# A graph network with sorted chains: held rows and running sums as scans over features in PSUM

## The chip, the cores and the metric

One core of a Trainium2 chip. The time is device time of the whole kernel in microseconds (us); smaller is better. Engines: TensorE (PE), VectorE (DVE), ScalarE (ACT), GpSimd (POOL), SyncE (SP, which only issues DMAs here).

## The reference, cut to what matters

6,250 nodes with 128 features, 100,000 edges sorted by destination. Four graph layers, each followed by a layer norm over nodes:

```python
# layer 0 ("first walk")
theta = x[dst] - x[src]
w = sigmoid(relu(theta @ W1 + b1) @ W2 + b2)
agg = segment_sum(w * theta, dst)
# layer 1: attention over edges grouped by source (needs the edges sorted by source: "sort" and "sorted pass")
# layer 2 ("transformer's walk"), 8 heads of 16
scores = sum(q[src] * k[dst], -1) / 4 + edge_attr @ We + be
ex = exp(scores - segment_max(scores, dst)[dst]); agg = segment_sum(v[src] * ex / den[dst], dst)
# layer 3: two graph attention layers, 4 heads of 32 ("attention walks")
```

## The kernel before, in words

**Chains.** Each of the 128 partitions holds 784 consecutive edges; a walk goes through them in 56 groups of 14 edges (`NG`, `B`). `cont[:, e]` is 1 where edge e has the same destination as the edge before it, otherwise 0. A segment sum is a running sum multiplied by `cont`: the sum at a node's last edge is the node's, and is fetched from `states` in HBM afterwards. A destination's row likewise is written by an indirect DMA at its first edge only (`spread_wide`, zero elsewhere) and *held* along the chain: held(e) = held(e-1) * cont(e) + row(e).

**A group of a walk.** POOL issues 14 indirect gathers, one per edge slot, each of 128 table rows into `rows` (L707), two groups in turn. It waits for `idx_staged` (ACT copies the indices, L1214) and for `rows_used` of the group two before. SP loads the group's spread rows into `dstf` (L580) once `dst_used` says that the held rows two groups back are made. DVE (function `turn`) computes scores, ACT the exponentials (and, in the first walk, 14 rows times their weight, L1196), DVE adds up, ACT saves the group's 14 rows of sums to `states` (L1223), two buffers in turn.

**First walk** (phase 0). DVE: subtract held - row, relu times W2 (one `stt`), from group `M0` = 20 on two bf16 one-hot compares for a histogram of sources (`mark_sources`), reduce; ACT exp; DVE 1/(1+..); ACT weighs row by row into `gated` in PSUM and tells `msg_ready` in parts; DVE then interleaves 14 adds into `sums` with 14 `hold` operations for the next group, each one `scalar_tensor_tensor` over 128 features that depends on the one before it:

```python
m = stt(S3[:, j, 0:A], prev, same_chain(g)[:, j:j + 1], part[:, j * A:(j + 1) * A], ALU.mult, ALU.add)
m = stt(held[:, j, :], prev, same_chain(g)[:, j:j + 1], dstf[:, s, j, 0:D], ALU.mult, ALU.add)
```

**Transformer's walk** (phase 2): the same with q*k product, reduce by head, two scans for the running maximum, exp on ACT, messages (v times exp, 136 wide with the denominators) into `msgp`, then the same 14 + 14 interleaved operations.

**Sort** (phase 1, `sort_edges`, `place_edges`, `hold_row`, ACT's `payloads`): for every group DVE builds bf16 one-hots (`build`), PE counts, DVE picks each edge's place, ACT copies the held rows (132 wide), weight and source number into `payload`, and POOL scatters 14 times 128 payloads to HBM (`by_src`, L634). It needs `payload_ready` and `place_ready`; ACT needs `sort_out`, the landing of the scatters of two groups before. DVE's hold operations for the next group stand among and behind the picks and wait for `held_copied`. After group 2 DVE also folds weights.

**Attention walks** (phases 3 and 4) already work the other way, and the change takes their form: a PSUM tile with the feature outside and the slot inside, 15 slots per feature (slot 0 the carry), a gate tile of the same shape with `cont` in slots 1 to 14 and 0 in slot 0, and one `tensor_tensor_scan` over all of it (L2057); ACT turns the result back into `sums` (L1217) and writes the next gate (L1179).

Line numbers of helpers in the profile: L1260 `tt`, L1268 `cp`, L1271 `stt`, L1274 `red`.

Of the kernel before, what the change touches and what calls it, by code (L numbers as in the profile page):

```python
# [7 lines left out]
ALU = mybir.AluOpType  # L8
# [56 lines left out]
def build(nc, a, out):  # L65
    with ExitStack() as ctx:  # L66
# [186 lines left out]
        gated = psA[:, 2 * D:(B + 2) * D]  # L253
# [3 lines left out]
        chain_exq = psA[:, 2048:2048 + 4 * (B + 1)]  # L257
        held = psA[:, 2048:2048 + B * D].rearrange("p (b d) -> p b d", d=D)
        heldS = psA[:, 0:B * ROW].rearrange("p (b d) -> p b d", d=ROW)
# [11 lines left out]
        w2p = psA[:, 2048 + B * D:2048 + B * D + D]  # L271
# [28 lines left out]
        gates_ready = sem("gates_ready")  # L300
        states_turned = sem("states_turned")
# [26 lines left out]
        base_ready = sem("base_ready")  # L328
# [7 lines left out]
        msg_ready = sem("msg_ready")  # L336
        hold_step = sem("hold_step")
# [101 lines left out]
        MSG_PARTS = [1, 5, 9, 13]  # L439
# [283 lines left out]
        def _(pe):  # L723
# [88 lines left out]
            for ph in range(5):  # L812
# [114 lines left out]
                if ph == 0:  # L927
                    pe.matmul(psX[:, 0:F], chains[0][:, :], last[:, 0:F], start=True, stop=True).then_inc(st_carry, 1)
# [18 lines left out]
        def _(act):  # L947
# [40 lines left out]
            def payloads():  # L988
# [3 lines left out]
                act.wait_ge(src_in, 48)  # L992
                for g in range(NG):
# [4 lines left out]
                    act.activation(payload[:, s, :, 0:ROW].rearrange("p b (h d) -> p b h d", d=33)[:, :, :, 0:32],  # L998
                                   heldS[:, :, 0:D].rearrange("p b (h d) -> p b h d", d=32), ACT.Copy)
                    act.activation(payload[:, s, :, ROW:ROW + 4], heldS[:, :, D:ROW], ACT.Copy).then_inc(held_copied, 1)  # L1000
# [38 lines left out]
            for ph in range(6):  # L1039
# [133 lines left out]
                else:  # L1173
                    act.wait_ge(rows_used, 2 + TURN[ph] * NG)
                    for s in range(2):
                        act.activation(idx[:, s, :], src[:, s * B:(s + 1) * B], ACT.Copy).then_inc(idx_staged, 1)
                def chain_gates(g):
# [3 lines left out]

                if ph >= 3:
                    act.wait_ge(n_stage, KG * (ph + 1))
                    act.wait_ge(n_kept, 3 * KG)
                    chain_gates(0)
                for it in range(IT if ph != 1 else 0):
                    for s in range(2):
                        g = it * 2 + s
                        act.wait_ge(scores_ready, g + (1 + ph * NG))
# [1046 lines left out]
```

## Time and profile before

| | |
|---|---|
| median of 3 runs | 6638.7 us (6636.5 to 6639.4) |
| the profiled execution | 6635.3 us, span 6633.5 us |
| DVE / POOL / ACT / PE busy | 4655 / 4292 / 1376 / 1265 us |
| first walk, first to last gather | 244 to 1254 us |
| sort, first to last scatter | 1456 to 2473 us |
| transformer's walk | 3111 to 4098 us |
| attention walks | 4388 to 5374, 5533 to 6519 us |

DVE is the engine with the largest share; the stages named above follow one another, with node updates (gathers of sums, projections, layer norms) between them. An indirect DMA is counted as busy on POOL for the time in which POOL issues it.

### The profile page before, as it was taken

Reading aid. Unit: us, or ns where it says so; the run is one execution under the profiler, and the core shown is the slowest. Engines: PE = TensorE matmul, PEld = TensorE weight load, DVE = VectorE, ACT = ScalarE, POOL = GpSimd, SP = SyncE. Lnnn points to the kernel's source line nnn. Section 1 sums busy time; section 2 is a strip of 40 time slices with the busy share of each in tenths; the row PEclk is TensorE's granted clock in tenths of the full one; section 3 lists DMA queues with packets and bytes.
Section 4 is the critical chain, followed back from the end, with each engine's and each line's share of the span. In section 5 each row is a group of like instructions: output and inputs, shape, how many; then the busy total and the mean of one; then the engine's idle time right before and its main releaser. Section 6 shows DMA issues by size and latency. Waiting matters only on the chain. (4 is left out here: it accounts for less than half of the span.)

```text
span 6633.5 us, 37157 instructions
## 1 busy us (share of the span) xinstructions
PE 1264.7 (19%) x8049; PEld 1104.1 (17%) x8049; DVE 4654.6 (70%) x9454; ACT 1375.5 (21%) x3580; POOL 4291.5 (65%) x4445
## 2 busy tenths in 40 slices
PE   7100000145555534332000000820000010000000
PEld 6100000134554433322000000620000010000000
DVE  7678888799999969976888887644444443444445
ACT  0122222221111114431000000522222211222223
POOL 0677777667777760016777775457777767777775
PEclk9655555555555555556555555855555555555555
DMA  9666666434444437744666665123333323333332
GB/s 373 188 211 211 202 202 202 136 102 132 134 132 134 132 115 293 294 174 132 219 217 221 221 219 169 32 72 109 114 109 111 113 79 90 109 112 111 109 114 82
DMA packets 338944, 1032.97 MB, mean 156 GB/s; under 512 B 100325, under 2 KB 163137, under 8 KB 331294
## 3 DMA queue, kind: packets, MB, share of 16 engines
q0 software_dynamic: 166752, 401.68, 21.2%
q1 hardware_dynamic: 116642, 342.34, 14.8%
q10 hardware_dynamic: 55324, 286.57, 12.0%
q8 instruction: 63, 1.03, 0.1%
q14 instruction: 163, 1.34, 0.1%
HBM read 602.97 MB, written 427.39 MB: 155 GB/s over the span
## 5 line engine op out<-in xcount | busy, mean ns | idle before, releaser
L707 POOL DMA_INDIRECT rows<-table,idx x3136 | 2986.7, 952 | 982.6 <-issue 972.2
L634 POOL DMA_INDIRECT by_src<-ebuf,place x784 | 771.0, 983 | 274.6 <-issue 238.4
L1271 DVE SCALAR_TENSOR_TENSOR psA<-psA,cont,dstf 128x128 f32<-128x128 f32 (+1 forms) x2349 | 836.5, 356 | 52.0 <-ACT ebuf L1000 31.3
L1260 DVE TENSOR_TENSOR sc<-rows,ebuf 128x56 f32<-128x56 f32 x112 | 28.2, 252 | 1023.5 <-DMA rows<-table,idx 1023.5
L933 PE MATMUL psA<-dstf,ones 128*128 128x512 f32 x10 | 9.9, 1113 | 3055.9 <-DVE dstf L2176 3055.9
L1271 DVE SCALAR_TENSOR_TENSOR sums<-sums,cont,psA 128x128 f32<-128x128 f32 (+1 forms) x1512 | 519.3, 343 | 30.5 <-ACT psA L1196 29.1
L933 PEld LDWEIGHTS psA<-dstf,ones 128*128 128x128 f32 x10 | 2.7, 315 | 3057.5 <-issue 3057.5
L802 PE MATMUL psA<-attr,sums 128*128 128x49 f32 x1568 | 406.0, 403 | 474.8 <-DVE attr L1449 474.8
L2057 DVE TENSOR_TENSOR_SCAN psA<-rows,psA 128x1980 f32<-128x1980 f32 x112 | 480.1, 4287 | 3.9
L802 PEld LDWEIGHTS psA<-attr,sums 128*128 128x128 f32 x1568 | 396.9, 326 | 480.9 <-DVE attr L1449 480.9
L1202 ACT ACTIVATE psA<-df 128x60 f32<-128x60 f32 (+1 forms) x168 | 40.4, 241 | 1714.5 <-DVE df L1260 1714.5
L1260 DVE TENSOR_TENSOR psA<-rows,psA 128x1848 f32<-128x1848 f32 (+1 forms) x168 | 352.7, 2100 | 0.0
L714 POOL DMA_INDIRECT fixr<-states,fixi x5 | 5.0, 998 | 518.3 <-DMA states<-sums 464.5
L653 POOL DMA_INDIRECT spread_wide<-rows,nidx x147 | 153.4, 1044 | 267.4 <-DVE rows L1260 219.4
L1260 DVE TENSOR_TENSOR rows<-rows,psA 128x1792 bf16<-128x1792 bf16 (+3 forms) x121 | 234.4, 1937 | 108.4 <-DMA rows<-table,idx 104.7
L645 POOL DMA_INDIRECT sums<-states,nidx x245 | 256.7, 1048 | 81.2 <-issue 73.1
L1260 DVE TENSOR_TENSOR rows<-psA,rows 128x1792 f32<-128x1792 f32 (+2 forms) x168 | 203.1, 1210 | 124.1 <-DMA rows<-table,idx 112.6
L1217 ACT ACTIVATE sums<-psA 128x1848 f32<-128x1848 f32 x112 | 191.7, 1711 | 460.0 <-DVE psA L2057 460.0
L998 ACT ACTIVATE ebuf<-psA 128x1792 f32<-128x1792 f32 x56 | 94.2, 1682 | 907.5 <-DMA by_src<-ebuf,place 788.1
L1196 ACT ACTIVATE psA<-rows,wt 128x128 f32<-128x128 f32 x784 | 232.9, 352 | 33.7 <-DVE wt L2077 33.7
L774 PE MATMUL psA<-ebuf 128*128 128x49 bf16 x504 | 54.4, 276 | 971.7 <-DVE ebuf L1260 971.7
L803 PEld LDWEIGHTS psA<-rows 128*128 128x128 bf16 x784 | 210.2, 268 | 0.0
(336 smaller groups left out, 5409.4 us busy)
## 6 DMA issues: line engine op xcount, KB each, us to landing
dstf<-spread_wide SPq DMA_DIRECT2D x168, 924.0 KB, 7.0
states<-sums ACTq DMA_DIRECT2D x150, 952.0 KB, 3.9
rows<-by_src SPq DMA_DIRECT2D x55, 1035.0 KB, 5.1
states<-sums ACTq DMA_DIRECT2D x56, 1008.0 KB, 5.8
spread_wide<-sums SPq DMA_DIRECT2D x56, 924.0 KB, 24.3
states<-sums ACTq DMA_DIRECT2D x56, 903.0 KB, 7.2
rows<-table,idx POOLq DMA_INDIRECT x3136
msg<-low_rows SPq DMA_DIRECT2D x56, 448.0 KB, 3.8
```

The lines of the kernel that those rows point to most:

```text
L634: pool.indirect_dma_start(by_src[:, :], bass.IndirectOffsetOnAxis(ap=place[:, s, j:j + 1], axis=0), payload[:, s, j, :], None).then_inc(so ...
L645: pool.indirect_dma_start(nrows[g % NS][:, b * w:(b + 1) * w], None, states[ph - 1][:, :], bass.IndirectOffsetOnAxis(ap=nidx[:, order, k:k ...
L653: pool.indirect_dma_start(spread[ph][:, :], bass.IndirectOffsetOnAxis(ap=nidx[:, 1, k:k + 1], axis=0), zslot(ph, g)[:, b * ZW[ph]:(b + 1) ...
L707: pool.indirect_dma_start(rows[:, at:at + GW[ph]], None, table[ph][:, :], bass.IndirectOffsetOnAxis(ap=idx[:, s, j:j + 1], axis=0)).then_i ...
L802: pe.matmul(t, hotT[s][:, j, :], cell[:, :, j], start=True, stop=False)
L803: m = pe.matmul(t, same[s][:, j, :], hotH[s][:, :, j], start=False, stop=True)
L998: act.activation(payload[:, s, :, 0:ROW].rearrange("p b (h d) -> p b h d", d=33)[:, :, :, 0:32], heldS[:, :, 0:D].rearrange("p b (h d) -> ...
L1196: m = act.activation(gated[:, j * D:(j + 1) * D], rows[:, at:at + D], ACT.Copy, scale=wt[:, s, j:j + 1])
L1217: act.activation(S3[:, :, 0:F], chain_msg.rearrange("p (f b) -> p b f", b=B + 1)[:, 1:B + 1, :], ACT.Copy).then_inc(states_turned, 1)
L1260: return dve.tensor_tensor(o_, a_, b_, op)
L1271: return dve.scalar_tensor_tensor(o_, a_, s_, b_, op0, op1)
L2057: tell(dve.tensor_tensor_scan(chain_msg, chain_gate, chain_msg, 0.0, ALU.mult, ALU.add), su)
```

## The change

In the first walk, the sort and the transformer's walk:

- `hold_row` and `hold` go. ACT copies the group's spread rows from `dstf` into a PSUM tile turned by feature (slots 1 to 14), after it has copied slot 14 of the group before into slot 0, and writes a gate from `cont`. DVE runs two scans, each over half the features.
- The 14 adds go. In the first walk ACT weighs its 14 rows straight into slots 1 to 14 of `first_acc`, and `msg_ready` in parts is gone: the sums begin when all 14 are weighed. In the transformer's walk DVE writes the messages turned. DVE adds up in two scans of half the features; ACT then turns the sums into `sums` in SBUF and only then saves them.
- In the first walk the order on DVE is: hold scans of the next group, then sum scans. In the transformer's walk the front half of the hold scans comes ahead of the messages, the back half behind the sum scans.
- The gates are bf16 in the walks (64 or 68 features x 15) and f32 in the sort (66 x 15). The transformer's exponentials lie in PSUM from column 3968, in its last bank.
- New waits: the histogram's matmuls wait for the states of the group before (`states_turned0`), and ACT's weighing waits for the histogram's matmuls.

```diff
-        gated = psA[:, 2 * D:(B + 2) * D]
+        wide_msg = psA[:, 0:(B + 1) * 136]
+        wide_held = psA[:, 2048:2048 + (B + 1) * D]
+        wide_exq = psA[:, 3968:3968 + 8 * (B + 1)]
+        acc_gate = msg[:, 0:(B + 1) * 34].bitcast(BF16)
+        hold_gate = msg[:, (B + 1) * 34:(B + 1) * 66].bitcast(BF16)
+        sort_held = psA[:, 0:(B + 1) * ROW]
+        first_held = psA[:, 0:(B + 1) * D]
+        first_acc = psA[:, 2048:2048 + (B + 1) * D]
...
                     pe.wait_ge(hist_ready, g + 1)
+                    pe.wait_ge(states_turned0, g)
...
+                def turn_held(g):
+                    act.wait_ge(dst_landed[g % 2], 16 + 16 * IT + 16 * (g // 2))
+                    if g:
+                        act.activation(view[:, :, 0], view[:, :, B], ACT.Copy).then_inc(hold_carried, 1)
+                        act.wait_ge(hold_carried, NG - 1 + g)
+                        act.wait_ge(held_copied, g)
+                        act.activation(view[:, :, 1:B + 1].rearrange("p f b -> p b f"), dstf[:, g % 2, :, :], ACT.Copy)
...
+                    act.activation(sort_gate.rearrange("p (f b) -> p f b", b=B + 1)[:, :, 1:B + 1],
+                                   cont[:, g * B:(g + 1) * B].unsqueeze(1).to_broadcast([P, 66, B]), ACT.Copy).then_inc(hold_turned, 1)
...
+                        if ph == 0 and g < NG - 1:
+                            turn_first(g + 1)
+                        if ph == 2 and g < NG - 1:
+                            turn_held(g + 1)
                         act.wait_ge(scores_ready, g + (1 + ph * NG))
...
+                            act.wait_ge(hist_used, max(g + 1, M0))
                             for j in range(B):
-                                m = act.activation(gated[:, j * D:(j + 1) * D], rows[:, at:at + D], ACT.Copy, scale=wt[:, s, j:j + 1])
-                                if j in MSG_PARTS[:-1]:
-                                    m.then_inc(msg_ready, 1)
+                                m = act.activation(acc_rows[:, :, j + 1], rows[:, at:at + D], ACT.Copy, scale=wt[:, s, j:j + 1])
...
+                        if ph == 0:
+                            act.wait_ge(sums_saved[s], it * 16 + 16)
+                            m = act.activation(sums[:, s * B * W:(s + 1) * B * W].rearrange("p (b w) -> p b w", b=B)[:, :, 0:D],
+                                               acc_rows[:, :, 1:B + 1].rearrange("p f b -> p b f"), ACT.Copy)
+                            if g < NG - 1:
+                                m = act.activation(acc_rows[:, :, 0], acc_rows[:, :, B], ACT.Copy)
+                            m.then_inc(states_turned0, 1)
+                            if g < NG - 1:
+                                first_gate(1, g + 1).then_inc(sum_gates, 1)
+                            act.wait_ge(states_turned0, g + 1)
...
+            def hold_turn(g):
+                half = 66 * (B + 1)
+                dve.wait_ge(hold_turned, NG + g + 1)
+                dve.tensor_tensor_scan(sort_held[:, 0:half], sort_gate, sort_held[:, 0:half], 0.0, ALU.mult, ALU.add)
+                dve.tensor_tensor_scan(sort_held[:, half:2 * half], sort_gate, sort_held[:, half:2 * half],
+                                       0.0, ALU.mult, ALU.add).then_inc(dst_used, 1)
...
                 cp(place[:, s, :], spot[:, :]).then_inc(place_ready, 1)
-                if held_next:
-                    for j in range(3, B):
-                        hold_row(holds, g + 1, j)
+                if g < NG - 1:
+                    hold_turn(g + 1)
...
+                            if ahead:
+                                hold_first(g + 1)
+                            dve.wait_ge(rows_used, g + 3)
+                            dve.wait_ge(sum_gates, g + 1)
+                            for k in range(2):
+                                m = dve.tensor_tensor_scan(halves_of(first_acc)[k], first_gates[1], halves_of(first_acc)[k], 0.0, ALU.mult, ALU.add)
+                            tell(m, su)
...
+                            if ahead:
+                                hold_front(g + 1)
+                            wide_messages(g, G3, Sp)
+                            if ahead:
+                                hold_back(g + 1)
```

## Rows read from the trace of the kernel before

**Rows 1.** The page: busy time, share of the span, instructions of each engine.

```profile
PE 1264.7 (19%) x8049; PEld 1104.1 (17%) x8049; DVE 4654.6 (70%) x9454; ACT 1375.5 (21%) x3580; POOL 4291.5 (65%) x4445
```

**Rows 2.** Windows by stage: stretch, length, engines' busy us (xcount), clock, DMA share, GB/s.

```profile
700.00:1200.00 500.00, 40.82 (x378) 35.01 (x378) 424.23 (x988) 126.68 (x434) 374.85 (x382) 0.50 0.61 201
1700.00:2400.00 700.00, 357.56 (x2716) 345.46 (x2716) 647.35 (x979) 77.56 (x156) 532.47 (x544) 0.50 0.41 134
3200.00:4000.00 800.00, 0.00 (x0) 0.00 (x0) 691.06 (x1626) 44.96 (x227) 601.49 (x636) 0.50 0.67 221
4500.00:5200.00 700.00, 0.00 (x0) 0.00 (x0) 311.76 (x315) 166.83 (x276) 526.34 (x559) 0.50 0.38 111
```

**Rows 3.** Lines, first walk: xcount, busy us, mean ns, idle before and its releasers.

```profile
L707 POOL DMA_INDIRECT rows<-table,idx x784 | 759.0, 968 | 251.0 <-issue 241.2 <-ACT idx L1214 7.6 <-ACT psA L1196 2.1
```

**Rows 4.** Timeline, first walk, group 25: start us, us, engine, line, tiles, idle before.

```profile
705.43 2.02 DVE L1260 TENSOR_TENSOR rows<-psA,rows 128x1792 f32<-128x1792 f32 x1 [1.32 <-DMA rows<-table,idx]
...
713.92 4.16 ACT L1196 ACTIVATE psA<-rows,wt 128x128 f32<-128x128 f32 x14 [0.59 <-DVE wt L2077]
...
721.84 0.33 ACTq L1223 DMA_DIRECT2D states<-sums  x1
...
723.36 2.03 DVE L1260 TENSOR_TENSOR rows<-psA,rows 128x1792 f32<-128x1792 f32 x1 [1.28 <-DMA rows<-table,idx]
```

**Rows 5.** Timeline, transformer's walk, two group starts on DVE.

```profile
3611.41 2.02 DVE L1260 TENSOR_TENSOR rows<-rows,psA 128x1792 f32<-128x1792 f32 x1 [7.57 <-DMA rows<-table,idx]
...
3627.36 2.02 DVE L1260 TENSOR_TENSOR rows<-rows,psA 128x1792 f32<-128x1792 f32 x1
```

**Rows 6.** Timeline, sort, one group of ACT and DVE.

```profile
1970.94 1.68 ACT L998 ACTIVATE ebuf<-psA 128x1792 f32<-128x1792 f32 x1 [16.85 <-DMA by_src<-ebuf,place]
...
1972.76 0.36 DVE L1271 SCALAR_TENSOR_TENSOR psA<-psA,cont,dstf 128x132 f32<-128x132 f32 x1 [1.62 <-ACT ebuf L1000]
...
1979.30 0.24 DVE L1268 TENSOR_SCALAR psA<-attr 128x49 f32<-128x49 f32 x1
...
1981.40 1.52 DVE L1260 TENSOR_TENSOR rows<-digits,ebuf 128x1792 bf16<-128x1792 bf16 x2
```

**Rows 7.** Sort: the waits (total us, times, longest), and the scatters by line.

```profile
DVE psA L1271 <- ACT ebuf L1000: 31.3, 42, 1.9
...
L634 POOL DMA_INDIRECT by_src<-ebuf,place x784 | 771.0, 983 | 274.6 <-issue 238.4 <-DVE place L1268 36.2
```

**Rows 8.** Timeline, POOL's issues beside the pair of one-hot compares, three places.

```profile
933.70 1.59 DVE L1260 TENSOR_TENSOR ebuf<-digits,ebuf 128x1792 bf16<-128x1792 bf16 x2
933.74 0.94 POOL L707 DMA_INDIRECT rows<-table,idx  x1 [0.30 <-issue]
...
1674.75 1.51 DVE L1260 TENSOR_TENSOR rows<-digits,ebuf 128x1792 bf16<-128x1792 bf16 x2
1674.80 1.86 POOL L634 DMA_INDIRECT by_src<-ebuf,place  x1 [0.30 <-issue]
...
1982.46 1.29 POOL L634 DMA_INDIRECT by_src<-ebuf,place  x1 [0.30 <-issue]
```

**Rows 9.** Timeline, sort, POOL waiting for place numbers.

```profile
1514.21 0.96 POOL L634 DMA_INDIRECT by_src<-ebuf,place  x1 [4.42 <-DVE place L1268]
```

**Rows 10.** Lines, attention walk, 4400 to 5370 us: two scans and ACT's turn.

```profile
L2057 DVE TENSOR_TENSOR_SCAN psA<-rows,psA 128x1980 f32<-128x1980 f32 x55 | 235.8, 4287 | 1.9
...
L1217 ACT ACTIVATE sums<-psA 128x1848 f32<-128x1848 f32 x55 | 94.1, 1711 | 225.9 <-DVE psA L2057 225.9
...
L2093 DVE TENSOR_TENSOR_SCAN fm<-nf,sc 128x60 f32<-128x60 f32 x55 | 15.5, 282 | 2.2 <-DVE sc L1271 0.4
```

**Rows 11.** Timeline, end of the first walk: weighing and save.

```profile
1266.00 4.16 ACT L1196 ACTIVATE psA<-rows,wt 128x128 f32<-128x128 f32 x14 [0.59 <-DVE wt L2077]
...
1272.59 0.33 ACTq L1223 DMA_DIRECT2D states<-sums  x1
```

**Rows 12.** Timeline, end of the transformer's walk: the dependent adds.

```profile
4109.33 5.06 DVE L1271 SCALAR_TENSOR_TENSOR sums<-sums,cont,psA 128x136 f32<-128x136 f32 x13
```

More of the change, by code:

```diff
@@ L438, in build @@
         XS = [1, 1, 1, 3, 1, 0]
-        MSG_PARTS = [1, 5, 9, 13]
         @block.sync
@@ L1201, in _ @@
                             n = H * (B + 1)
-                            act.activation((chain_exq if ph >= 3 else exq)[:, 0:n], df[:, 0:n], ACT.Exp).then_inc(weights_ready, 1)
+                            act.activation((chain_exq if ph >= 3 else wide_exq)[:, 0:n], df[:, 0:n], ACT.Exp).then_inc(weights_ready, 1)
                             act.wait_ge(sums_saved[s], it * 16 + (16 + 16 * IT * TURN[ph]))
@@ L1441, in build, with place_edges @@
                 dve.wait_ge(built, g + 3)
-            def place_edges(holds, g):
+            def place_edges(g):
                 s = g % 2
@@ L2009, in _ @@
                         link(dve.memset(chain_gate.rearrange("p (f b) -> p f b", b=B + 1)[:, :, 0], 0.0))
-                    link(dve.memset(held[:, B - 1, :], 0.0)) if ZW[ph] == ROW else None
-                    link(cp(w2p, bias[:, bb("L0_gnn_W2"), :])) if ph == 0 else None
+                    if ph == 2:
+                        for gate in (acc_gate, hold_gate):
+                            link(dve.memset(gate.rearrange("p (f b) -> p f b", b=B + 1)[:, :, 0], 0.0))
+                    if ph == 0:
+                        for gate in first_gates:
+                            link(dve.memset(gate.rearrange("p (f b) -> p f b", b=B + 1)[:, :, 0], 0.0))
+                        link(dve.memset(first_acc.rearrange("p (f b) -> p f b", b=B + 1)[:, :, 0], 0.0))
+                        tell(cp(w2p, bias[:, bb("L0_gnn_W2"), :]), hrd)
                     link(dve.memset(mx[:, :], 0.0))
@@ L2016, in _ @@
                 sr = Steps(scores_ready, NG * ph)
-                holds = Steps(hold_step, (B - 1) * NG * min(ph, 2))
-                accs = Steps(acc_step, (B - 1) * NG * ph)
-                parts = Steps(msg_ready)
+                mxd = Steps(held_read, NG + 1)
                 wide = int(ZW[ph] == ROW)
-                part, A = (msgp, F) if ph else (gated, D)
+                part, A = msgp, F
                 def same_chain(g):
                     return cont[:, g * B:(g + 1) * B]
-                def hold(g, j, first=False):
-                    s = g % 2
-                    prev = held[:, j - 1, :] if j else held[:, B - 1, :]
-                    if j:
-                        dve.wait_ge(hold_step, holds.value())
-                    if first and j == 0:
-                        m = cp(held[:, 0, :], zrow[:, 0:D])
-                    else:
-                        m = stt(held[:, j, :], prev, same_chain(g)[:, j:j + 1], dstf[:, s, j, 0:D], ALU.mult, ALU.add)
-                    if j < B - 1:
-                        m.then_inc(hold_step, 1)
-                        holds.add()
-                    else:
-                        m.then_inc(dst_used, 1)
-                        du.add()
                 def turned_messages(g, G3, Sp):
@@ L2136, in turn @@
-                        dve.wait_ge(sums_ready, su.value())
-                        if wide and ahead:
-                            dve.wait_ge(dst_used, du.value())
+                            if ahead:
[3 more added lines that the diff above has]
+                                hold_back(g + 1)
                 wr = Steps(weights_ready)
@@ L2145, in _ @@
                         link(ts(hb(nf)[:, :, 1:B + 1], same_chain(0).unsqueeze(1).to_broadcast([P, H, B]), -1.0, ALU.add, BIG, ALU.mult))
-                    if wide:
-                        dve.wait_ge(dst_landed[0], 16 + 16 * IT * ph)
-                        dve.wait_ge(zfirst_in, 16 * (ph + 1))
-                        for j in range(B):
-                            hold(0, j, first=True)
-                        dve.wait_ge(dst_used, du.value())
+                    if ph == 2:
+                        hold_front(0)
+                        hold_back(0)
+                    if ph == 0:
+                        hold_first(0)
                     for it in range(IT):
@@ L2168, in _ @@
                     continue
-                if ph >= 3:
-                    dve.wait_ge(states_turned, (ph - 2) * NG)
+                dve.wait_ge(states_turned, (ph - 1) * NG) if ph > 1 else None
                 if ph > 1:
```

185 lines of the change are left out of this document (111 added, 74 removed).

## The prediction, made before the change was run

> **What bounds the kernel now.** I read the page's engine shares first: DVE is busy for 70% of the span, GpSimd (POOL) for 65% [rows 1]. That points at DVE; the windows by stage correct it [rows 2]. POOL issues 636 gathers in 800 us of the transformer's walk and 559 in 700 us of an attention walk: 1.258 and 1.252 us each, so 14 of them, a group, take 17.5 to 17.6 us. The rate is the same where DVE is busy for 86% and for 45%. In the first walk from group 20 on it is 1.309 us, in the sort 1.287. The listing by line agrees: of 251.0 us in which POOL stands idle in the first walk, 241.2 are its own 0.30 between issues [rows 3]. So POOL's issue of 14 indirect DMAs a group sets the pace of all these stages, and DVE's share is high only because its work nearly fills that time.
>
> How nearly, the timeline tells. In the first walk DVE starts a group at 705.43, ends its adds at 721.8 and its last held row 0.26 later, and waits 1.3 us for the rows of the next at 723.36 [rows 4]: a chain of 16.7 us in 17.9. Before group 20 the pair of histogram compares (1.3 us) is missing: 15.4. In the transformer's walk the chain is 15.95 us (3611.41 to 3627.36) [rows 5]. In the sort, groups come every 18.0 us (1.287 x 14) and DVE waits in 42 of them, 0.75 us each, for ACT's payload copies [rows 7]: a chain of about 17.2. ACT in turn had waited 16.85 us for scatters of two groups earlier to land [rows 6]; so POOL leads there too.
>
> What slows POOL in two stages is visible as well. An undisturbed issue takes 0.96 us in the sort and 0.946 in the walks, the mean is 0.983 and 0.968: over 784 issues 18 to 20 us and 17 us [rows 3, 7]. The long ones lie under the pair of bf16 one-hot compares, DVE instructions with both inputs in SBUF, and their price hangs on where POOL stands when the pair starts [rows 8]: an issue that falls 1.06 us behind the pair's start (1982.46 behind 1981.40) takes 1.29, one 0.05 us behind takes 1.86, one 0.04 us behind takes 0.94. So the price climbs to 0.90 as the issue comes nearer to the start, and falls off an edge between 0.05 and 0.04. The Trainium skill (SBUF — State Buffer, section Who interferes with whom) infers that a tensor_tensor takes only the shared read interface and leaves descriptor writing alone; by that these delays would be 0 wherever the pair starts. The rows show 0.90, so I go by the rows. A third loss: POOL once waits 4.42 us for DVE's place numbers behind the weight folds [rows 9], and 9.7 us for ACT in the first walk, a few times about 2 [rows 3].
>
> **The change, part by part.** Scan cost first: 1,980 elements take 4.287 us, 60 take 0.282 [rows 10], so 2.086 ns an element and 0.157 us fixed; 960, 990 and 1,020 elements take 2.16, 2.22 and 2.28 us, and two with no wait between them overlap by 0.08. ACT: 1,848 elements in 1.711 us, 128 every 0.30 [rows 4, 10]: 0.82 ns each and 0.19 fixed. A turn of 1,792 elements takes 1.68, a gate of 896 0.93, of 924 0.95, of 952 0.97, a carry 0.30. An ACT instruction starts 0.1 before the end of an independent one ahead of it.
>
> *First walk.* DVE loses 28 row operations, 7.4 us at a spacing of 0.26, and gains four scans of 960 elements, 4.23 + 4.23 us. The chain to the weights stays (713.92, +8.5) [rows 4]. ACT turns the next destination rows under the compares and the reduce: held tile free at +4.1, carry, turn and gate 2.9, done at +7.1, before the scores at +7.6. Hold scans run +8.7 to +12.9, while ACT weighs 14 rows (4.16, done at +12.65), sum scans to +17.2. Chain 17.2 us against 17.9: hidden, by 0.7. Before group 20 the scores are there at +6.2 but ACT at +7.1, so the exponential comes 1.0 later: 15.4 + 0.5 + 1.0 = 16.9 against 17.5, hidden. POOL needs the rows freed by +15.9 (its next group ends 17.8 us after the last gather, rows land 1.9 after it); they are free at +12.7. The added waits: the next subtract stands behind the hold scans (+12.9), the histogram matmuls behind the previous turned states, ACT's weighings behind those matmuls (done by +7.2, needed at +8.5), the save of states behind a turn, a carry and a gate. The save goes out 3 us later, the destination load 4 us earlier than now (both at 721.8 to 722.1 [rows 4]); gathers that land beside both come late (7.57 us of waiting [rows 5]). I take 0 for that; bounds: POOL's waits for ACT go (-6 to -10), or later landings shift the compares' price in 36 groups by -0.3 to +0.4 us (-11 to +14).
>
> The last group has no cover. Now the adds begin with the first weighed row, and the save leaves 6.6 us after the weights, at 1272.59 [rows 11]. After: 4.16, two scans 4.23, turn 1.68 and 0.1 of waits, 10.2 in all: **+3.7 us**, on the path, since POOL waits for that save.
>
> *Transformer's walk.* Hold front (2.16) starts when the maxima are done at +5.6 and also covers the 0.44 of waiting for the exponential; then carry product, messages 2.14, two scans of 1,020 (4.48), hold back 2.16: 5.6 + 2.2 + 0.2 + 2.2 + 4.5 + 2.2 = 16.9 us against 17.6, hidden by 0.7. ACT's turn of the held rows ends at +5.1, before +5.6. At the end, 14 dependent adds of 5.4 us [rows 12] become scans of 4.48 and a turn of 1,904 elements, 1.76: **+0.9 us**.
>
> *Sort, start and stall.* The copy and 13 dependent holds (5.5 us at the spacing of [rows 12]) become two scans of 990 (4.36) behind an ACT turn that fits under build(0): -0.8, if the load has landed. In each group DVE loses three interleaved rows and eleven dependent ones and gains 4.36 us: 17.2 becomes 16.7, place numbers come 0.4 earlier within the group. The first scatter waits for DVE and so does the one behind the stall [rows 9]: 0.8 + 3 x 0.5 + 0.4, **-2.7 us**.
>
> *Sort, steady part.* DVE keeps ahead of POOL, but the place where its cycle is tied to POOL moves. Now: scatters land, ACT starts the payload at 1970.94 (call it T), DVE resumes at T+1.82 and the compares start at T+10.46 [rows 6]. After: the payload's four copies end at T+2.0, the carry at T+2.2, the turn of 1,848 at T+3.9, the gate at T+4.8; DVE T+4.9, scans 4.36, cell copy T+9.3, compares 2.10 later as in [rows 6], at T+11.43: 0.97 us later. POOL's beat of 1.26 stays, so the issue that now falls 1.06 behind the compares' start will fall 0.09 behind it: just short of the edge, where the price is 0.86 instead of 0.33. Of some 47 steady groups I take 35 at 0.84, 12 beyond the edge at 0.3, and 8 early ones at 0.5: 37 us against today's 19, **+18 us**. Bounds: all beyond the edge, 11 us (-9); all short of it, 45 (+25).
>
> Sum: +3.7 - 2.7 + 18 + 0.9 = +19.9 us. The profiled execution took 6635.3 us (span 6633.5), 3.4 under the median of 6638.7; it becomes 6655, the median **6658 us**.
>
> The skill (VectorE: DVE Perf Modes, section The TRN2 errata) says that small VectorE operations pay a fixed cost each and recommends 512 elements or more, which speaks for 4 instructions instead of 28. Here the scans' 2.09 ns an element eats that up, and with POOL in front neither would move the end.
>
> **Rivals.** (B) *The compares slip past the edge.* It needs the sort's ACT chain to be 0.05 us longer than I have it. Collisions 11 us instead of 19, all else as above: +1.9 - 9 = -7, median 6632; with groups on either side, up to +13. For: how little separates 0.09 from 0.04. Against: the chain is built from measured durations. (C) *ACT or DVE becomes the bound in a walk.* If ACT's copies into a PSUM tile with a step of 15 elements take twice as long (+1.7 us), the exponential of the first walk and hold front of the transformer's come about 1.2 us late: chains of 18.0, 18.4 and 18.1 against 17.5, 17.95 and 17.6, so 20 x 0.5 + 36 x 0.45 + 56 x 0.5 = 54 us on the forecast, 6712; it decides above 0.6 us more a group. Against: reading PSUM with that step is at full rate (1.711 for 1,848 [rows 10]). (D) *Faster:* gathers no longer land beside save and load together. POOL's waits go (-6), later landings slip the histogram's compares past their edge (36 x 0.3 = -11), the sort's slip too (-9), with -2.7 and +4.6: -24 us, 6615. It decides once landings shift by 0.5 us. Against: two independent slips. (E) *Nothing measurable:* the collisions stay: +1.9, 6641.
>
> **How the numbers follow.** A measurement of this kernel tells 0.2%, 13 us, from no change. My forecast case has 0.55, of which 0.44 lies above +13 and 0.11 below; B and E together 0.30, within; C 0.07, slower; D 0.08, faster. So faster 0.08, same 0.41, slower 0.51. The forecast case alone runs from +5 to +32 (6644 to 6671); for eight in ten I reach down over B and up into C: 6629 to 6682.
>
> **What would show it.** Right: issues still every 1.25 us with 0.30 idle; DVE chains near 17.2, 16.9 and 16.7 us; mean scatter near 1.005 us instead of 0.983, with an issue about 0.1 us behind the compares' start; save of the last first-walk group 3.7 us later behind its weights; the stall of 4.42 some 2 us shorter. Wrong: DVE without waits for rows over whole stretches (C); mean scatter at 0.98 or below (B, E); mean gather of the first walk under 0.96 and no wait of POOL for ACT (D).

## The result, and the profile after the change

The changed kernel takes 6653.9 us (median; 6647.3 to 6657.5), the kernel before 6638.1 on the same chip: a ratio of 1.0023, 95% interval 1.0017 to 1.0029. The profiled execution spans 6652.9 us instead of 6633.5: **+19.4 us**, where the sum of the prediction had +19.9. For this pair of executions the sum is right to half a microsecond, its terms are not; the medians differ by 15.8 us.

The page after the change, and the windows over the stretches of [rows 2] in the same columns:

```profile
PE 1263.5 (19%) x8049; PEld 1102.1 (17%) x8049; DVE 4744.1 (71%) x6098; ACT 2140.7 (32%) x4363; POOL 4298.5 (65%) x4445
```

```profile
700.00:1200.00 500.00, 42.35 (x392) 36.30 (x392) 443.70 (x326) 276.36 (x597) 372.01 (x381) 0.50 0.61 201
1700.00:2400.00 700.00, 353.61 (x2677) 341.62 (x2677) 625.25 (x501) 181.55 (x266) 535.42 (x534) 0.50 0.41 131
3200.00:4000.00 800.00, 0.00 (x0) 0.00 (x0) 744.95 (x545) 293.25 (x455) 601.53 (x635) 0.50 0.67 220
4500.00:5200.00 700.00, 0.00 (x0) 0.00 (x0) 312.14 (x315) 167.27 (x280) 526.84 (x559) 0.50 0.38 111
```

DVE issues 3356 instructions fewer and is busy for 90 us more (a scan of 960 elements costs 2.14 us); ACT is busy for 765 us more. In the transformer's walk DVE goes from 691 to 745 us of 800, and POOL still issues 635 gathers there (636 before). What changed in time is read from the starts and ends of POOL's first and last issue of each stage:

| stage | before, us | after, us | difference |
|---|---|---|---|
| ahead of the first walk | 244.4 | 246.0 | +1.6 |
| first walk, 784 gathers | 1009.6 | 1018.0 | +8.4 |
| last gather to the fix of the chunk ends | 22.9 | 24.9 | +2.0 |
| from there to the first scatter | 178.8 | 177.5 | -1.3 |
| sort, 784 scatters | 1016.9 | 1025.5 | +8.6 |
| transformer's walk, 784 gathers | 987.3 | 987.1 | -0.2 |
| all the rest | 3173.6 | 3173.9 | +0.3 |

*The sort.* One steady group in the timeline, ACT, DVE and POOL (start, us, engine, line, tiles, idle before); the answer to [rows 6]:

```profile
2054.44 1.69 ACT L1027 ACTIVATE ebuf<-psA 128x1792 f32<-128x1792 f32 x1 [13.85 <-DMA by_src<-ebuf,place]
...
2056.65 1.71 ACT L1013 ACTIVATE psA<-dstf 128x1848 f32<-128x1848 f32 x1
2058.30 0.96 ACT L1018 ACTIVATE rows<-cont 128x924 f32<-128x924 f32 x1
...
2047.15 1.52 DVE L1357 TENSOR_TENSOR rows<-digits,ebuf 128x1792 bf16<-128x1792 bf16 x2
...
2059.29 2.23 DVE L1513 TENSOR_TENSOR_SCAN psA<-rows,psA 128x990 f32<-128x990 f32 x1 [1.99 <-ACT rows L1018]
...
2065.98 1.51 DVE L1357 TENSOR_TENSOR rows<-digits,ebuf 128x1792 bf16<-128x1792 bf16 x2
...
2046.06 0.95 POOL L643 DMA_INDIRECT by_src<-ebuf,place  x1 [0.30 <-issue]
2047.32 1.76 POOL L643 DMA_INDIRECT by_src<-ebuf,place  x1 [0.31 <-issue]
```

The payload starts at 2054.44 (T), the scans at T+4.85, the compares at T+11.54; predicted were 4.9 and 11.43 (over the steady groups the compares start at T+11.36 in the median, in the kernel before at T+10.47). In the group before, the compares start at 2047.15 and the next issue falls 0.17 behind and takes 1.76. Of 40 steady groups (from 1700 us on) 28 have this issue 0.07 to 0.18 behind the compares, at 0.79 to 0.91 us above the undisturbed 0.96. The line of the scatters and POOL's stall, against [rows 7, 9]:

```profile
L643 POOL DMA_INDIRECT by_src<-ebuf,place x784 | 781.3, 997 | 271.8 <-issue 238.5
...
1522.73 0.95 POOL L643 DMA_INDIRECT by_src<-ebuf,place  x1 [2.63 <-DVE place L1365]
```

997 ns instead of 983 over 784 scatters are the sort's +10.3 us, and the stall gives back 1.8.

*The first walk.* A group start, and POOL's longest waits at groups 9, 18, 27, 36, 45 and 54, each ahead of the third gather:

```profile
712.55 2.02 DVE L1357 TENSOR_TENSOR rows<-psA,rows 128x1792 f32<-128x1792 f32 x1 [1.09 <-DMA rows<-table,idx]
...
408.54 0.95 POOL L716 DMA_INDIRECT rows<-table,idx  x1 [2.86 <-issue]
...
569.00 0.94 POOL L716 DMA_INDIRECT rows<-table,idx  x1 [3.25 <-issue]
732.77 0.94 POOL L716 DMA_INDIRECT rows<-table,idx  x1 [4.18 <-issue]
899.23 0.94 POOL L716 DMA_INDIRECT rows<-table,idx  x1 [3.84 <-issue]
1065.49 0.94 POOL L716 DMA_INDIRECT rows<-table,idx  x1 [3.89 <-issue]
...
1230.22 0.94 POOL L716 DMA_INDIRECT rows<-table,idx  x1 [3.83 <-issue]
```

The same six waits are in the kernel before, at 1.21 to 1.31 us (one of them below), and in the transformer's walk of both, at about 1.3; in the attention walks they take 1.0 to 1.1.

```profile
725.20 0.94 POOL L707 DMA_INDIRECT rows<-table,idx  x1 [1.25 <-issue]
```

In the first walk of the changed kernel they grew by 14.3 us together, while the waits for ACT went from 9.7 to 5.6 (the first walk's line: mean gather 966 ns, idle 260.5 us instead of [rows 3]'s 251.0). Nothing in the prediction names this pause.

### The profile page after: what moved, and what is told of

Same layout as the page of the kernel before. It is cut to its first block and busy times, and to the rows that moved or that the text cites. A ratio compares the mean times of both kernels' runs of the same rounds, so it can differ in the third digit from the quotient of the medians.

```text
span 6652.9 us, 34825 instructions
## 1 busy us (share of the span) xinstructions
PE 1263.5 (19%) x8049; PEld 1102.1 (17%) x8049; DVE 4744.1 (71%) x6098; ACT 2140.7 (32%) x4363; POOL 4298.5 (65%) x4445
## 3 DMA queue, kind: packets, MB, share of 16 engines
q14 instruction: 145, 1.19, 0.1%
## 5 line engine op out<-in xcount | busy, mean ns | idle before, releaser
L2160 DVE TENSOR_TENSOR_SCAN psA<-msg,psA 128x960 f32<-128x960 bf16 x112 | 234.5, 2140 | 8.0 <-ACT msg L1210 8.0
L2192 DVE TENSOR_TENSOR_SCAN psA<-msg,psA 128x960 f32<-128x960 bf16 x112 | 234.1, 2136 | 3.9 <-ACT psA L1280 3.9
```

The source lines that it names most:

```text
L2160: m = dve.tensor_tensor_scan(halves_of(first_held)[k], first_gates[0], halves_of(first_held)[k], 0.0, ALU.mult, ALU.add)
L2192: m = dve.tensor_tensor_scan(halves_of(first_acc)[k], first_gates[1], halves_of(first_acc)[k], 0.0, ALU.mult, ALU.add)
```

## The experiments

Times are medians beside the kernel before on the same chip. "Sort" is the time from the first scatter's start to the last's end, "first walk" the same of its gathers.

| run | us | before | ratio (95%) | first walk | sort | mean scatter, ns |
|---|---|---|---|---|---|---|
| the change | 6653.9 | 6638.1 | 1.0023 (1.0017 to 1.0029) | 1018.0 | 1025.5 | 997 |
| e1, gate early | 6630.1 | 6636.7 | 0.9991 (0.9982 to 1.0000) | 1012.5 | 1009.5 | 977 |
| e2, 0.08 us later | 6647.9 | 6636.7 | 1.0017 (1.0008 to 1.0026) | 1014.1 | 1025.9 | 997 |
| e3, load late | 6638.8 | 6636.7 | 1.0004 (0.9995 to 1.0013) | 1004.6 | 1025.3 | 997 |
| e4, half the descriptor space | 6687.6 | 6636.7 | 1.0077 (1.0062 to 1.0092) | 1016.1 | 1035.3 | 998 |
| e5, gate early, turn in three | 6631.1 | 6639.6 | 0.9988 (0.9979 to 0.9997) | 1016.0 | 1003.9 | 969 |
| e6, turn in three | 6636.5 | 6639.6 | 0.9995 (0.9986 to 1.0004) | 1016.2 | 1008.4 | 975 |
| e7, e5 and e3 | 6619.4 | 6639.6 | 0.9970 (0.9957 to 0.9982) | 1005.3 | 1004.8 | 970 |
| e8, before, one copy split | 6632.0 | 6639.6 | 0.9989 (0.9980 to 0.9998) | 1013.6 | 1008.9 | 973 |

**What sets the price of the sort's scatters?** First the gate is moved ahead, so that the compares start earlier:

```diff
+                    if g < NG - 1:
+                        held_gate(g + 1)        # ahead of the payload copies
...
                     if g < NG - 1:
                         turn_held(g + 1)        # the turn alone
```

> After the change, with ACT's gate of the sort's next group written as soon as DVE's scans of this group are done, ahead of the payload copies instead of behind the turn. Theory (the place of the compares on POOL's beat sets the price of an issue): the compares start about 0.85 us earlier in each steady group, so the issue that follows them falls about 0.95 instead of 0.1 us behind their start; by the prices of the two traces that is 0 to 0.33 us a group instead of 0.80 to 0.90. Mean scatter 0.97 to 0.983 instead of 0.997, 6640 to 6645 us, 9 to 14 below the change. Rival (the scans themselves, or the gates that they read from SBUF, slow the scatters): mean scatter stays at 0.997 and the time within 3 us of the change.

A steady group of e1, compares and the issues beside them:

```profile
2034.68 1.52 DVE L1364 TENSOR_TENSOR rows<-digits,ebuf 128x1792 bf16<-128x1792 bf16 x2
...
2034.55 0.96 POOL L643 DMA_INDIRECT by_src<-ebuf,place  x1 [0.30 <-issue]
2035.81 1.22 POOL L643 DMA_INDIRECT by_src<-ebuf,place  x1 [0.30 <-issue]
```

The sort is 16.0 us shorter and the scatters' mean is 977: the theory holds, the rival (scans or gates slow the scatters) falls, since both are still there. The compares moved 0.89 us earlier behind the payload's start (median), and the issue now falls 1.13 us behind their start instead of 0.17. The median is 10 us below the range that was expected. In the profiled executions the other 5.5 us come from the first walk, which e1 doesn't touch. So that walk varies from run to run: five runs with the change's own first walk (the change, e1, e2, e5, e6) gave 1012.5 to 1018.0, mean 1015.4, and the two with that of before 1009.6 and 1013.6. By these means the walk's +8.4 would be nearer to +4.

Then the other way, by one more small ACT copy ahead of the turn (e2), and by splitting the turn (e6):

```diff
+                        act.activation(...sort_gate..., [:, 0:1, 1:B + 1], ... cont ..., ACT.Copy)      # e2
```

```diff
-                        act.activation(view[:, :, 1:B + 1]..., dstf[:, g % 2, :, :], ACT.Copy)
+                        for f in range(0, ROW, 44):                                                   # e5, e6, e7
+                            m = act.activation(view[:, f:f + 44, 1:B + 1]..., dstf[:, g % 2, :, f:f + 44], ACT.Copy)
```

> After the change, with one more small ACT copy (the gate's first feature written twice, 14 elements, 0.1 to 0.2 us) between the payload and the turn of the sort's held rows. Theory of the place on the beat: the compares start 0.1 to 0.2 us later, past the start of the next issue; the issues that cost 0.80 to 0.90 in some 28 groups cost about 0.16 to 0.33: mean scatter 0.97 to 0.98, 6636 to 6643 us, 11 to 18 below the change although only work was added. Rival (the chain over ACT and DVE is what costs): the time is the change's or up to 10 us above, since each group gets 0.15 us longer.

> The change with the gate where the change has it and the turn of the sort's held rows in three copies, 0.16 to 0.2 us later than the change, about twice what one small copy added (0.08 us, which left the next issue 0.05 to 0.07 us behind the compares' start, still short of the edge, at 0.89). Theory of the place on the beat: now the issue starts just ahead of the compares, price 0.16 to 0.24 instead of 0.8 to 0.9: mean scatter 0.970 to 0.980, 10 to 16 us below the change's 6652: 6636 to 6642 us. Rival (the longer chain costs): 6652 to 6660 us.

One group of e2, then one of e6:

```profile
2045.12 1.52 DVE L1360 TENSOR_TENSOR rows<-digits,ebuf 128x1792 bf16<-128x1792 bf16 x2
...
2045.19 1.85 POOL L643 DMA_INDIRECT by_src<-ebuf,place  x1 [0.30 <-issue]
```

```profile
2038.73 1.53 DVE L1358 TENSOR_TENSOR rows<-digits,ebuf 128x1792 bf16<-128x1792 bf16 x2
...
2038.72 0.96 POOL L643 DMA_INDIRECT by_src<-ebuf,place  x1 [0.30 <-issue]
2039.98 1.12 POOL L643 DMA_INDIRECT by_src<-ebuf,place  x1 [0.30 <-issue]
```

e2's expected gain did not come: the copy moved the compares by 0.08 us only, the issue fell 0.07 behind them, short of the edge, and took 1.85; the sort stayed at 1025.9, and the total, 6647.9, missed the expected 6636 to 6643. e2 doesn't tell the two theories apart, e6 does. In e6 the turn takes 1.90 us instead of 1.71 and the compares move by 0.19: the issue starts 0.01 us ahead of the compares and goes free, the one behind it pays 0.16, and the sort is **17.1 us shorter with work added** to the chain that releases DVE. That is rival B of the prediction made real: its "edge" lies where the trace of before showed it, and the sort's collisions add up to 13 us, where B had 11.

Last, toward the place where no issue pays, in the change (e5) and in the kernel before (e8):

```diff
-                    act.activation(payload[:, s, :, ROW:ROW + 4], heldS[:, :, D:ROW], ACT.Copy).then_inc(held_copied, 1)
+                    act.activation(payload[:, s, :, ROW:ROW + 2], heldS[:, :, D:D + 2], ACT.Copy)
+                    act.activation(payload[:, s, :, ROW + 2:ROW + 4], heldS[:, :, D + 2:ROW], ACT.Copy).then_inc(held_copied, 1)   # e8
```

> The gate written early as before, and the turn of the sort's held rows in three ACT copies of 44 features instead of one of 132, which adds 0.16 to 0.2 us to ACT's chain ahead of the scans. With the early gate alone the compares start 0.14 us behind the start of an issue in most steady groups, and the next issue costs 0.27 more; at 0.22 to 0.35 the two traces show no price. Theory of the place on the beat: added work brings them there, mean scatter 0.958 to 0.966 instead of 0.977, another 8 to 14 us off the early gate's 6630: 6616 to 6622 us. Rival (a shorter chain is what paid): the time is the early gate's or up to 10 us above it.

> The kernel before, with the second payload copy of the sort (4 features a row) in two copies of 2, some 0.08 to 0.1 us more on ACT ahead of DVE's held rows. In the kernel before, the compares start 0.20 us behind the start of an issue in most steady groups, at a price of 0.33, and from 0.22 on there is none. Theory of the place on the beat: mean scatter 0.965 to 0.972 instead of 0.983, 8 to 14 us below the kernel before: 6622 to 6630 us. Rival: same as before or a few us above.

A group of e5, and one of e8:

```profile
2036.68 1.52 DVE L1365 TENSOR_TENSOR rows<-digits,ebuf 128x1792 bf16<-128x1792 bf16 x2
...
2037.61 0.99 POOL L643 DMA_INDIRECT by_src<-ebuf,place  x1 [0.30 <-issue]
```

```profile
2038.00 1.55 DVE L1261 TENSOR_TENSOR rows<-digits,ebuf 128x1792 bf16<-128x1792 bf16 x2
...
2039.01 0.96 POOL L634 DMA_INDIRECT by_src<-ebuf,place  x1 [0.31 <-issue]
```

e8's group is free of the price, e5's pays 0.03. The sorts are 1003.9 and 1008.9 us, 5.6 below e1 and 8.0 below the kernel before. The means, 969 and 973, miss what was expected by a few ns: the 14 early groups, in which POOL starts with the place numbers in hand, keep their own places and pay up to 0.9 each; most of e5's steady groups still pay 0.02 to 0.05; and in both kernels three groups right behind a short pause of POOL (0.75 us, every 161 us) pay 0.8, since the pause shifts the beat. Both totals miss their ranges too: 6631.1 instead of 6616 to 6622, which is where the rival had e5, and 6632.0 instead of 6622 to 6630. e5's median does not show the gain over e1 and e8's profiled span is not below that of the kernel before, because their first walks took 3.5 and 4.0 us longer (in e8 the work ahead of it 3.6 more); the gain is read from the sort alone. e8 is the control that matters for the change: a split of one copy gives the old kernel 0.11%, interval 0.02 to 0.20. By e6 and e8, most of what the change costs in the sort is where its compares fell on POOL's beat, not the work that it moved.

**What lengthens the pauses of the first walk?** SP's queue, load of destination rows:

```diff
                         sp.wait_ge(dst_used, g + 1 + ph * NG)
+                        if ph == 0 and g > 2:
+                            sp.wait_ge(states_turned0, g - 2)
```

> After the change, with SP's load of a later group's destination rows in the first walk made to wait for the states of the group before, so that load and save are issued together again, as before the change. Theory (load and save apart keep the gathers' transfers late, and POOL's pause once in nine groups waits for them): row landings lag 2 us again, the six pauses of 2.9 to 4.2 us fall to about 1.3, first walk 10 to 14 us shorter, 6640 to 6645 us. Rival (the later reads and frees of rows in the chain over ACT and the scans cause the pauses, the load has no part in it): pauses stay near 3.7, time within 3 us of the change.

The change first, then e3: issue of the load and the save of one group (timeline) and their landing times in us (DMA issues, 700 to 1200 us); for e3 a pause as well:

```profile
707.40 0.32 SPq L589 DMA_DIRECT2D dstf<-spread_wide  x1
...
713.36 0.33 ACTq L1320 DMA_DIRECT2D states<-sums  x1
...
dstf<-spread_wide SPq DMA_DIRECT2D x27, 924.0 KB, 4.8
states<-sums ACTq DMA_DIRECT2D x27, 903.0 KB, 4.1
```

```profile
1054.99 0.32 SPq L591 DMA_DIRECT2D dstf<-spread_wide  x1
...
1054.95 0.35 ACTq L1322 DMA_DIRECT2D states<-sums  x1
...
1055.88 0.94 POOL L718 DMA_INDIRECT rows<-table,idx  x1 [1.22 <-issue]
...
dstf<-spread_wide SPq DMA_DIRECT2D x27, 924.0 KB, 7.8
states<-sums ACTq DMA_DIRECT2D x27, 903.0 KB, 7.0
```

Shown: the two transfers, 6 us apart in the change, are together again; all six pauses are 1.20 to 1.27, and the walk takes 1004.6 us, 8 to 13 below the runs with the change's walk and 5 below the kernel before. The rows of a group land 1.7 to 2.0 us behind POOL's last gather throughout; in the change this lag is 2 us right behind a pause and 3.4 to 4.7 us at the end of each nine groups (at most 5.2). The load and the save themselves land later together (7.8 and 7.0 us) than apart (4.8 and 4.1): the transfers that got faster are not the ones that POOL waits for. Why gathers beside one stream at a time fall behind, and not beside both, stays open. (The median, 6638.8, is just below the range that was expected.)

```profile
4572.55 0.94 POOL L716 DMA_INDIRECT rows<-table,idx  x1 [2.13 <-issue]
```

The pauses come every 112 gathers instead of every 126, six in a walk as before, at 2.4 us instead of 1.3 in the transformer's walk, at 2.1 instead of 1.0 to 1.1 in the attention walks (the row is one) and at 3.1 to 5.2 in the first; the whole is 34 us longer than the change. So the pause does depend on this space, and the rival falls; but half the space should have halved the distance, and it did not: it made each pause longer. Nor does the count run on from stage to stage: with the full space it is the 129th gather of every walk that pauses first, whatever was issued before the walk. How the space is laid out stays open.

**Do the parts add up?** e7 has the early gate, the turn in three and the late load.

> The early gate, the turn in three copies and the late load of destination rows in the first walk, together. If the parts are independent the gains add up (late load 12 us, the other two 22 and some 10): 6606 to 6614 us, below the kernel before by 0.35 to 0.5%. If they share a cause (both only shift the same beat), the gain is that of the larger: 6616 to 6622 us.

6619.4 us, 0.30% below the kernel before (interval 0.18 to 0.43%) and the fastest measured. First walk and sort are each those of e3 and e5 within 1 us, so the parts are independent. By the number alone the other expectation would have won (6616 to 6622), for the sum was put together from gains that were too large: it took 22 us for e1, part of which was the first walk's scatter, and 10 more for e5, which its median did not show. Beside the kernel before, e3 and e5 are 13.7 and 24.3 us better than the change, and e7 36.0, 2 us short of their sum.

**Is DVE near to being the bound, and can the first walk's compares be placed?** Two runs added a reduction to each group of the transformer's walk in the changed kernel (its result is read by nobody), two moved the histogram's compares behind the scores' reduction in e7:

```diff
                             if ahead:
                                 hold_back(g + 1)
+                            link(red(pad[:, 0:1], bias[:, 0:4, :]...))          # e10; 0:12 in e11
```

```diff
-                            if g >= M0:
-                                dve.wait_ge(hist_used, g)
-                                mark_sources(g)
                             tell(red(ex[:, s * B:(s + 1) * B], G1), sr)
+                            if g >= M0:                                         # e9, e12
+                                dve.wait_ge(hist_used, g)
+                                mark_sources(g)
```

> After the change, with one more DVE instruction in every group of the transformer's walk (a sum over 512 constant elements into a column that nothing reads, about 0.65 us with its semaphore) behind the held rows' second scan. Theory (POOL's issue sets the pace, DVE's chain of 16.8 has 0.8 us to spare): chain 17.5, idle of DVE 0.9 falls to about 0.25, the walk stays at 987 us, time within 5 us of the change. Rival (DVE is the bound, since it is busy for 86% and more of this walk): 56 x 0.65 = 36 us longer.

> The same with a sum over 1536 elements, about 1.8 us a group. Theory (0.8 us to spare, beyond it all counts): chain 18.6 us, walk 56 x 18.6 = 1042 instead of 987, 50 to 60 us above the change. Rival (DVE is the bound throughout): 56 x 1.8 = 100 us above it. Rival (POOL has further slack, DVE is nowhere the bound): within 5 us.

> All three edits of the run before (early gate, turn in three copies, late load), and the histogram's pair of compares in the first walk behind the reduction of the scores instead of ahead of it. There the compares start 0.71 to 0.85 us behind the start of a gather's issue in 29 of 35 groups, price 0.39 to 0.54, and 1.09 to 1.11 in 6, price 0.77. Theory of the place on the beat: the reduction takes 2.01 us, so they start 2.05 later, which is 0.80 on a beat of 1.25: 0.26 to 0.40 behind, where the price is 0 to 0.1. Mean gather of the first walk 0.950 to 0.955 instead of 0.970, first walk 10 to 16 us shorter. Against it: the histogram's matmuls end some 1.6 us later, ACT weighs later and DVE's chain grows from 17.2 to about 17.6, near the 17.5 that POOL then needs, which can give back up to 6 us. Sum 6604 to 6614 us. Rival (prices belong to the compares wherever they are): mean gather 0.970, 6619 to 6625 us.

> The kernel of the run with the compares behind the reduction, once more, since that run and its kernel before were on a chip that takes 7551 us for the kernel before. There DVE's chain from group 20 on was 17.75 us, with 1.1 us of waiting for ACT's weighing behind the later histogram matmuls. So on a chip that takes 6640 for the kernel before: mean gather of the first walk 0.950 to 0.958 instead of 0.970, but DVE's chain of 17.75 now sets the pace from group 20 on instead of POOL's 17.5, against 17.95 a group before: 36 x 0.2 = 7 us off the run with early gate and late load, 6609 to 6616 us. Rival (the prices go with the compares): 0.970, and 6619 to 6625 us.

All four were on two other chips, on which the kernel before takes 7551 and 7682 us and ACT waits up to 12.9 us at a time for something that the profile only calls remote. Their totals (e10 7453, e11 7470, e9 7395, e12 7475) say nothing about these theories. All four are below the kernel before there, by 1.1 to 2.7%, even the change with work added (e11: ratio 0.9893, 0.9864 to 0.9922), so the +0.23% of the change holds for chips like that of the first row of the table; why the others differ was not found. In the transformer's walk the trouble begins at group 14, so its first groups can be read. DVE in e10 and e11:

```profile
3730.15 0.66 DVE L1372 TENSOR_REDUCE pad<-bias 128x1 f32<-128x512 f32 x1
3731.08 2.02 DVE L1358 TENSOR_TENSOR rows<-rows,psA 128x1792 f32<-128x1792 f32 x1 [0.26 <-DMA rows<-table,idx]
```

```profile
3712.74 2.02 DVE L1358 TENSOR_TENSOR rows<-rows,psA 128x1792 f32<-128x1792 f32 x1
...
3731.11 2.02 DVE L1358 TENSOR_TENSOR rows<-rows,psA 128x1792 f32<-128x1792 f32 x1
...
3870.63 0.94 POOL L717 DMA_INDIRECT rows<-table,idx  x1 [1.25 <-issue]
```

With 0.66 us more, DVE still waits 0.26 us for the rows, and POOL's groups 1 to 9 come every 17.51 us (17.50 in the change). With 1.73 more, DVE goes from group to group in 18.37 us without a wait, falls 0.85 a group behind POOL until both slots of rows are full, and then POOL waits for it: 1.01 us ahead of group 9 and 1.25 ahead of groups 12 to 16 (the last row), where 0.30 is usual. From group 9 to 13 POOL's period is 18.40 (17.81 in the change; both have a pause there). So the slack that the prediction took, 0.7 us, was 0.8, and beyond it all counts; for a whole walk this wasn't measured.

For the compares behind the reduction, DVE's chain was 17.79 us where it had no other wait, 1.1 of it waiting for ACT's weighing, which waits for the later histogram matmuls. As a group takes 18.0 us in e7, at most 36 x 0.2 = 7 us were to be had. The place that was aimed at was not reached: with groups paced by these waits, the issues started 0.32 or 0.72 us behind the compares in e9 and paid 0.63 or 0.22, and the mean gather was 967 and 966 ns (e9, e12), not the 950 to 958 expected. Whether the compares can be placed on a chip like that of e7 stays open.

## Why the prediction was right, and where it wasn't

- **POOL's issue is the bound**: right. DVE's chains came out at 16.99 us (17.2 predicted, first walk), 16.2 ahead of group 20 (16.9) and 16.81 (16.9, transformer's walk); the transformer's walk did not change (987.3 and 987.1), and e11 shows DVE's bound 0.8 us away. Rival C (ACT's strided copies at twice the time) had nothing behind it: the turn of 1792 elements takes 1.67 us.
- **The sort's collisions, +18**: the mechanism was right to 0.1 us in place (issue 0.09 behind predicted, 0.07 to 0.18 measured; price 0.86 against 0.79 to 0.91), the sum was too large: +10.3. One reading of it was wrong, though the sum puts no group where it matters: the price does not climb steadily from 0.33 at 1.06 us, it is zero from 0.96 to 1.04 and the 0.33 belongs to the second compare (table below). The step that failed is the count, "35 at 0.84, 12 beyond the edge at 0.3, and 8 early ones at 0.5". Measured: 28 steady and 2 early groups at 0.79 to 0.91, the other 12 steady ones at 0.11 to 0.50, and 8 of the 14 early ones at 0.11 to 0.17. Why fewer groups sat there than counted was not tested.
- **Sort start and stall, -2.7**: -1.3 and -1.8.
- **End of the first walk, +3.7**: from the start of the weighing to the save 10.13 us (10.2 predicted; 1274.42 to 1284.55) against 6.59 in [rows 11], so +3.5 (and 10.2 less 6.6 is 3.6, not the sum's 3.7). Of that +2.0 reached POOL, since in the kernel before DVE started the last group late: 3.5 us behind POOL's last gather instead of 2.0, as it was still at work on the group before when the rows had landed (1.8 us behind that gather).
- **End of the transformer's walk, +0.9**: from DVE's first product to the save 14.65 us against 13.90 in the kernel before, +0.75; but that product began 0.2 us sooner behind the last gather, and the next step followed the save 0.3 us sooner, so +0.2 reached POOL.
- **The moved load and save, "I take 0 for that"**: this step was wrong. The bounds (-10 to +14) held, but they came from other causes, POOL's waits for ACT (-4.1, right in sign) and slips of the compares' price (-1.3 by the mean gather). The cost was the pause once in nine groups, +14.3 in this execution, visible in the trace of before at 1.3 us six times and nowhere in the prediction; e3 shows that the moved load causes it.

So +19.9 for +19.4 is luck, mainly two errors that cancel: 7.7 us too many in the sort, 8.4 too few in the first walk. The first walk alone varies by 5.5 us between runs with the same code for it, and the medians differ by 15.8, not 19.4.

## What to carry to other kernels

Where two engines run on locked beats and contend for a moment, read from the trace at which offset they meet and what each offset costs, before judging an edit by the work that it saves: here 0.19 us more work on ACT took 17 us off the sort, and 0.9 us of delay had cost it 10. Where a tuned kernel moves a bulk transfer that is "hidden", look for every wait that its move can lengthen (here POOL's pause), not only for its own consumer. And a change that ends slower can hold the faster kernel: with its offsets set, e7 beats the kernel before by 0.30%.

## What the runs showed of the hardware

**How long POOL's issue is held by a compare.** Over nine traces (the kernel before, the change, e1 to e3, e5 to e8) an indirect DMA's issue that starts while a bf16 compare with both inputs in SBUF is running ends 0.81 to 0.84 us after that compare ends. The first of the pair runs for 1.09 us, the second for 0.51:

| issue starts behind the first compare's start, us | issues | issue takes, us | ends after the end of that compare |
|---|---|---|---|
| -0.05 to 0.05 | 63 | 0.94 to 0.96 (57 of them), 1.86 to 1.88 (6, all from 0.044 on: the edge) | |
| 0.05 to 0.15 | 76 | 1.76 to 1.87 | 0.81 to 0.84 |
| 0.45 to 0.55 | 90 | 1.36 to 1.46 | 0.81 to 0.83 |
| 0.85 to 0.95 | 80 | 0.96 to 1.08 | 0.82 to 0.84 |
| 0.96 to 1.04 | 47 | 0.94 to 0.96 (not held) | |
| 1.05 to 1.15 | 95 | 1.19 to 1.30 (held by the second) | 0.81 to 0.84 (the second's) |

An issue of 0.96 us that starts just ahead of the compare is not held. So the price is what is left of the compare, less some 0.1 us: at most 0.9, zero in the last 0.15 us of the first, and again up to 0.33 in the second. In the change's trace other DVE instructions with two SBUF inputs hold issues too. The norm's `rows<-rows,X` in f32 does: four issues that start 0.08 to 0.10 behind it take 1.81 to 1.83. So do scans, and each issue ends 0.75 us after the scan's end: all 72 beside `ebuf<-cont,dstf` (1.79 us long, nine traces) take 1.52 to 2.27. The first and the third of four such scans, merged in one row, and two of the issues beside them:

```profile
4413.81 7.27 DVE L2079 TENSOR_TENSOR_SCAN ebuf<-cont,dstf 128x784 f32<-128x784 f32 x4
...
4416.66 1.52 POOL L716 DMA_INDIRECT rows<-table,idx  x1 [0.30 <-issue]
4418.48 1.52 POOL L716 DMA_INDIRECT rows<-table,idx  x1 [0.30 <-issue]
```

The maxima's short scan (0.41 us long) does it as well, but costs at most 0.15 us, to an issue that starts within 0.2 us behind it; of 43 beside it most start later, and the median is 0.946. Beside scans and products with an operand in PSUM and beside reductions the issue stays at 0.944 to 0.958 us in the median (over 2000 issues). The Trainium skill (SBUF — State Buffer, section Who interferes with whom) says that a DVE instruction with two SBUF inputs contends with a GpSimd instruction that reads SBUF; the trace agrees. It infers beside it that descriptor generation is spared by a tensor_tensor; these rows say otherwise.

**POOL's pause** comes every 126 indirect DMAs with 32768 bytes of descriptor space and every 112 with 16384; it takes 1.2 to 1.3 us in the first walk where the gathers land 2 us behind their issue, and up to 4.2 where they lag by 4 or 5. Within a walk the distance is constant; from one walk to the next the count starts anew.
